# Both output products of a pair directly behind each other, and both additions to x together

## The reference

```python
h = layernorm(x) * (1 + ca) + sa                 # modulated by a condition vector
x = x + ga * attention(h)                        # 16 heads of 64, latent projections, rope on q and k
h = layernorm(x) * (1 + cb) + sb
x = x + gb * moe(h)                              # 8 experts, the best one or two by softmax scores, relu
# attention: h normalised again, c_q = h wdq^T, c_kv = h wdkv^T, q, k, v from them by head,
# softmax(q k^T / 8) v, all heads side by side times w_out^T, plus h
```

## Time and profile before

| what | value |
|---|---|
| median of 3 runs | 899.38 us (898.97 to 901.64) |
| the profiled execution's own time | 900.41 us |
| its span | 898.7 us |
| TensorE busy | 807.5 us, 90% of the span |
| VectorE, GpSimd, ScalarE busy | 633.1, 664.6, 391.1 us |
| granted TensorE clock, mean | 0.947 |

### The profile page before, as it was taken

The page is one execution under the profiler, slowest core; times in us unless marked ns, Lnnn a source line. Parts: engine busy times, 40 slices in busy tenths (PEclk is TensorE's granted clock), DMA queues, the critical chain, the costliest instruction groups (busy, mean ns, idle before and its releaser), DMA issues.

```text
span 898.7 us, 14641 instructions
## 1 busy us (share of the span) xinstructions
PE 807.5 (90%) x5118; PEld 484.9 (54%) x5118; DVE 633.1 (70%) x1141; ACT 391.1 (44%) x635; POOL 664.6 (74%) x348
## 2 busy tenths in 40 slices
PE   4779999999999999999999999999997967677771
PEld 2535555555555555555655555655553533377671
DVE  8987777778787878777777787777776548634122
ACT  3554444444444444444444444444543233254340
POOL 2579998999997979797978787878778545623213
PEclk8969999999999999999999999999999888979886
DMA  9100010101010101010110101010101000186872
GB/s 242 33 1 13 13 37 2 37 1 36 3 36 2 36 2 37 2 36 6 32 25 13 26 13 25 13 27 1 25 1 25 1 2 24 59 268 220 264 232 80
DMA packets 84089, 43.90 MB, mean 49 GB/s; under 512 B 57392, under 2 KB 73136, under 8 KB 83952
## 3 DMA queue, kind: packets, MB, share of 16 engines
q1 hardware_dynamic: 82992, 40.86, 17.8%
q0 software_dynamic: 1024, 2.10, 0.8%
HBM read 36.51 MB, written 6.16 MB: 47 GB/s over the span
## 4 chain that ended last, share of the span: by engine, by line
PE 80%; DVE 8%; DMA 4%; issue 3%; POOL 2%; ACT 1%; SPq 1%; POOLq 0%; DVEq 0%
PE ps_o L467 25%; PE ps_m L432 9%; PE ps_x L420 8%; PE ps_s L451 6%; PE ps_s L457 6%; PE ps_s L453 6%; PE ps_s L455 6%; PE ps_s L494 4%; PE ps_s L605 2%; DMA moe<-xs_dram 2%; PE ps_s L476 2%; PE ps_s L614 2%; DVE mx L1114 1%; DVE hn L1205 1%; POOL xs_dram L970 1%
## 5 line engine op out<-in xcount | busy, mean ns | idle before, releaser
L956 POOL TENSOR_TENSOR acc<-acc,probs 128x1024 f32<-128x1024 f32 (+1 forms) x192 | 462.7, 2410 | 107.4 <-ACT probs L716 86.5
L1114 DVE TENSOR_REDUCE mx<-ps_m 128x2 f32<-128x1024 f32 x240 | 293.8, 1224 | 105.2 <-PE ps_m L432 104.7
L716 ACT ACTIVATE probs<-ps_s 128x1024 f32<-128x1024 f32 x256 | 248.9, 1024 | 162.1 <-PE ps_s L457 161.9
L467 PE MATMUL ps_o<-probs,c_all 128*64 128x512 f32 x1024 | 251.6, 613 | 0.0
L432 PE MATMUL ps_m<-k_hi,q_hi 64*128 64x512 f32 x480 | 107.7, 444 | 8.1 <-DVE mx L1114 8.1
L467 PEld LDWEIGHTS ps_o<-probs,c_all 128*64 128x64 f32 x1024 | 62.9, 137 | 95.2 <-issue 45.5
L451 PE MATMUL ps_s<-q_hi,k_hi 64*128 64x512 f32 x512 | 102.0, 394 | 1.3 <-ACT probs L716 1.2
L453 PE MATMUL ps_s<-q_hi,k_lo 64*128 64x512 f32 x512 | 100.9, 389 | 0.0
L457 PE MATMUL ps_s<-neg_row,one_row 64*128 64x512 f32 x512 | 100.9, 389 | 0.0
L455 PE MATMUL ps_s<-q_lo,k_hi 64*128 64x512 f32 x512 | 100.6, 388 | 0.0
L432 PEld LDWEIGHTS ps_m<-k_hi,q_hi 64*128 64x128 f32 x480 | 46.5, 184 | 94.1 <-issue 83.3
(11 more groups left out here) (299 smaller groups left out, 1001.1 us busy)
## 6 DMA issues: line engine op xcount, KB each, us to landing
probs<-in_experts SPq DMA_DIRECT2D x15, 578.0 KB
rr<-rd_dram SPq DMA_DIRECT2D x62, 128.0 KB
wu<-in_wqk SPq DMA_DIRECT2D x16, 256.0 KB, 2.6
neg_row<-nm SPq DMA_DIRECT2D x256, 0.5 KB, 2.0
w_first<-in_experts SPq DMA_DIRECT2D x5, 578.0 KB
rot<-in_experts SPq DMA_DIRECT2D x5, 578.0 KB
hT<-in_experts SPq DMA_DIRECT2D x5, 578.0 KB
xs_dram<-zero SPq DMA_DIRECT2D x2, 960.0 KB, 9.8
```

What stands on the lines that cost most here:

```text
L467: ins = nc.tensor.matmul(ps_o[64 * h:64 * h + 64, :], c_all[:, (p // HP) * TB + kt, :], probs[:, st % 4, h, :], start=(kt == 0), stop=(kt ...
L716: nc.scalar.activation(probs[:, st % 4, :, :], ps_s[:, 2 * (st % 2):2 * (st % 2) + 2, :], ACT.Exp, scale=SCALE).then_inc(s["probs"], 1)
L956: V.tensor_tensor(acc[:, buf(p, half), heads, :], first, probs[:, st % 4, heads, :], ALU.add).then_inc(s["added"], 1)
L1114: V.reduce_max(mx[:, :, kh, qt], max_banks(q, n), AX.X).then_inc(s["max_reduced"], 1)
```

## The change

The first half's output product leaves group 4, the second's leaves group 6, and both stand in group 5, directly behind each other. The first is written to bank 2 and the second to bank 3, where both used bank 3 before. One wait for the exponential (that of step 11) stands for two (steps 9 and 13). Both additions to x move to the head of VectorE's group 6, from the heads of groups 5 and 7. Step 13 waits for both additions, where steps 11 and 15 waited for one each. The second half's division moves from VectorE's group 5 to group 4. In pair 15, `find_slots` is in VectorE's group 5 still, so that the first addition, which stood ahead of it, now stands behind it. The orders of ScalarE, GpSimd and SyncE are the same as before.

```diff
@@ score
-                if p > 0 and st in (11, 15):
-                    pe.wait_ge(s["out_added"], n_part(p - 1, st == 15))
+                if p > 0 and st == 13:
+                    pe.wait_ge(s["out_added"], n_part(p - 1, 1))
@@ TensorE, the loop over pairs and groups
-                    if p > 0 and g in (0, 4, 6):
+                    if p > 0 and g in (0, 5):
                         pe.wait_ge(s["probs"], n_step(p, 2 * g + 1))
...
-                    if p > 0 and g == 4:
-                        outputs(p - 1, 0, ps_s[:, 3, :])
-                    if p > 0 and g == 6:
+                    if p > 0 and g == 5:
+                        outputs(p - 1, 0, ps_s[:, 2, :])
                         outputs(p - 1, 1, ps_s[:, 3, :])
@@ VectorE, the loop over pairs and groups
-                    if g == 5 and p >= 1:
-                        out_add(p - 1, 0, ps_s[:, 3, :])
-                    if g == 7 and p >= 1:
+                    if g == 6 and p >= 1:
+                        out_add(p - 1, 0, ps_s[:, 2, :])
                         out_add(p - 1, 1, ps_s[:, 3, :])
...
                         if g == 3:
                             divide(p - 1, 0)
-                        if g == 5:
+                        if g == 4:
                             divide(p - 1, 1)
```

## The result

The changed kernel takes 905.19 us (median of 21 runs, 901.39 to 907.96), the kernel before 899.38 in as many runs beside it. The ratio is 1.0054, with a 95% interval of 1.0041 to 1.0067: slower by about 4.9 us (3.7 to 6.0), where 1.7 us less were forecast. The profiled execution of the changed kernel took 902.53 us of its own time with a span of 900.4, so it is one of the faster ones of the 21. Its first 103 us took 3.2 us less than those of the profiled execution of before (pair 1 begins at 103.1 instead of 106.3); the change does not touch that stretch. So the two traces are compared stretch by stretch, not by their ends.

The account below looks back on a forecast made before the run. TensorE's own instructions were taken to bound the middle pairs. Terms of -2.5 (pairs 1 to 13), -0.3 (pair 14) and +1.1 (pair 15) sum to -1.7 us: 897.7 from the median 899.38, with an 8-in-10 range of 895.7 to 901.6.

Parts of the forecast that it names:

- The products: Pairs 1 to 13, group 5: two products in a row cost 1.99 us instead of 2.18, saving 2.5 us in all.
- The wait for the additions in middle pairs: Pairs 1 to 13, step 13: the addition ends 0.47 us before the scores waiting for it, so nothing is lost.
- The division in group 4: Pairs 1 to 13, end of VectorE's group 4: the moved division takes 0.69 us of idle time and costs nothing.
- rival 4: Pairs 1 to 13: both additions run late, after the second product; 0.5 us lost per pair, 904.2 us; chance 0.05.
- Pair 14: Pair 14: the products' saving of 0.19 us and the division moved into idle time together save 0.3 us (0 to 0.5).
- The last pair: Pair 15: step 13 waits for additions behind `find_slots`, TensorE idles 2.2 to 3.5 us; 1.1 us lost (0.5 to 2.4).
- rival 1: Pair 15: TensorE's clock falls after the new idle stretch, costing 2 to 4 us more; 900.7 us, up to 902; chance 0.25.
- the late step: Pair 15, step 15: it starts at 772.8 instead of 771.95, 0.9 us late, at most 2.2.

## Why the prediction was wrong

- **The products (forecast -2.5 us): right.** Two in a row cost 1.98, 1.99 forecast. With the division out of the way a pair takes 43.23 instead of 43.43, so 0.20 × 13 = 2.6 us are there to be had. That the 0.19 saved is a first load that nothing hides was argued; no run tested it.
- **The wait for the additions in middle pairs (0): right.** No idle time ahead of step 13.
- **The division in group 4 (0): wrong, the first failed step.** The text said that it is "0.69 us of VectorE in a group that has lost nothing but time in hand", and backed it with VectorE's idle time before the addition. In the kernel before that idle time does stand at the end of VectorE's group 4, but only because VectorE waits there for the addition, while TensorE's product of group 4 runs. The change takes this product away, and the idle time moves with it behind group 5's work. At the end of group 4 the next reduction follows at once, and behind it TensorE's second maxima product has the 0.25 us in hand of which rival 4 spoke. The price was wrong as well: the division took 1.23 us there and not 0.69. It cost 0.28 us per pair in group 5 (7.30 against 7.02), 4.0 in thirteen with what pair 13 lost besides. The kernel before with the same move (43.43) and the changed one without it (43.29) show that it takes both the move and the missing product.
- **Pair 14 (-0.3): wrong in sign, by less than 1 us.** The group that waited for the slow division is faster by 0.33 in the kernel that moves only it, so that saving is real. But the wait for the normalisation grew, since its first eight operations took 7.62 us instead of 7.13. The ten traces with changed middle pairs all have 7.57 to 7.62, the three without 7.12 to 7.20. From pair 14's start to group 5 of pair 15, with the 1.09 of a moved product added, the three take 88.8 to 88.9 us and the ten 89.2 to 90.3; the changed kernel takes 89.4 in both of its traces. So 0.5 us are lost where 0.3 were to be gained. The half clock at the long waits of this stretch lasts 23.9 us in both traces, the changed kernel's and that of before; why the ten differ among each other stays open. The text had named "VectorE's normalisation at the pair's end" as what may give part back, and its range ended at 0.
- **The last pair (+1.1): right as a mechanism, and too small.** Group 6 would start at 765.5 and step 13 at 768.8 by the text, 10.1 us after group 5's start; it was 10.2. The idle stretch was forecast as 2.2 us and was 1.92, and `find_slots` as 4.0 and was 4.00. Two terms were missing or too small. One is rival 1: the clock fell behind 1.92 us of idle time, and that cost 1.6 us. The other is GpSimd's two additions in a row, 0.67 us instead of 0.2. The prediction's own rows give more than 0.2: an addition takes 1.79 us and the exponential that feeds the next one 0.97. With the 0.9 for the late step that makes 3.2. The traces have 3.1 for the kernel that changes only the last pair, and its ratio 3.0.
- **The chances.** Rival 1 had 0.25 and was half right: alone it would have given 899.3. Its price was 2 to 4 us and not 1.6, and its sign, `pv` at 3.6 us, did not come either, since two steps took 2.99. The text said that no row shows a gap of this length; the trace of before has one of 3.53 us (42.58 to 46.11), with half clock behind it. None of the rivals held the division, so the range ended 3.6 us under the result. Rival 4 gave 904.2, and its sign, a pair above 43.4, did come (43.52). But its mechanism, late additions, did not: that its number lies near the result is luck.
- **The parts together.** Pairs 1 to 13 give -2.6 + 4.0 = 1.4, pair 14 with the first groups of pair 15 gives 0.5, and the last pair from group 5 on 3.3: 5.2 us. From pair 1's first scores to the end of GpSimd's last addition the traces have 669.8 us before and 675.0 in both of the changed kernel, 5.2 more as well; the runs say 4.9 (3.7 to 6.0).

## What to carry to other kernels

A move that takes work from the bounding engine at one place also takes the cover under which other engines worked there; each operation that is moved at the same time must be checked against the new, shorter gap, and at the price it has there beside its neighbours, not at the one it had. In a pipeline whose last turn carries extra work, work out that turn apart: an addition behind five microseconds of small operations is harmless only as long as nothing waits for it. A movable operation goes well ahead of the result that is needed last: between the two reductions the division was at its slowest and cost nothing.

## What the runs showed of the hardware

- TensorE's clock fell to 0.50 behind an idle stretch of only 1.91 to 1.94 us, in all four traces that have it in the last pair, and in neither of the two where matmuls filled it. The half clock lasted 3.4 us. In the trace of before an idle stretch of 1.17 us left the clock at 1.00. The length of the idle time alone does not decide: early in the changed kernel's trace the clock fell at 61.7 in an idle stretch of 1.41 us (60.58 to 62.00), and one of 1.42 us in the trace of before (65.18 to 66.60) left it at 1.00.
- The Trainium skill, "SBUF — State Buffer", section "SBUF: two separate sides", describes exclusive use of the ports that VectorE and GpSimd share. The same division of 512 columns took 0.68, 1.07, 1.23 and 1.42 us in middle pairs, by the place where it stood beside GpSimd's work. These agree with that rule in kind; which of GpSimd's operations blocks it when, no run here was made to show.
- One float32 matmul of 512 columns with 128 rows and 128 output partitions, made of two passes, costs 0.91 us of TensorE at full clock (3.63 us for four).
